# Global attention: three banks for the maximum ring, one bank for the values' sums, and score steps in halves

## The reference

```python
q = _split_heads(x @ Wq + bq, h); k = ...; v = ...
pattern = jnp.einsum('bhid,bhjd->bhij', k, q) * scale
prob = jax.nn.softmax(pattern, axis=-2)
out = jnp.einsum('bhis,bhid->bhsd', prob, v)
return concat @ Wo + bo
```

## Time and profile before

| | |
|---|---|
| time, median of 3 runs | 5361.09 us (5356.98 to 5364.1) |
| profiled execution, its own time | 5343.82 us |
| its span | 5342.2 us |
| TensorE busy | 4731.0 us (89%) |
| VectorE busy | 3525.2 us (66%) |
| GpSimd busy | 2700.6 us (51%) |
| ScalarE busy | 2177.9 us (41%) |

### The profile page before, as it was taken

The page is one execution under the profiler, slowest core; times in us unless marked ns, Lnnn a source line. Parts: engine busy times, 40 slices in busy tenths (PEclk is TensorE's granted clock), DMA queues, the critical chain, the costliest instruction groups (busy, mean ns, idle before and its releaser), DMA issues.

```text
span 5342.2 us, 67966 instructions
## 1 busy us (share of the span) xinstructions
PE 4731.0 (89%) x21552; PEld 2824.3 (53%) x21552; DVE 3525.2 (66%) x4540; ACT 2177.9 (41%) x3392; POOL 2700.6 (51%) x1140
## 2 busy tenths in 40 slices
PE   5899999999999598788859999999999985987978
PEld 3455555555454375566634555555555543765656
DVE  4878778778775553454467787787787755544544
ACT  2334434434433264355323343344344333643553
POOL 0456556556557264255205565565565562642652
PEclk8999999999999798999979999999999997988989
DMA  1000000000000100000010000000000001000000
GB/s 39 5 5 1 5 5 1 5 5 1 5 2 1 52 1 33 17 1 2 32 35 5 5 1 5 5 1 5 5 1 5 2 1 52 1 33 17 1 33 16
DMA packets 78786, 59.19 MB, mean 11 GB/s; under 512 B 41304, under 2 KB 75392, under 8 KB 78464
## 3 DMA queue, kind: packets, MB, share of 16 engines
q1 hardware_dynamic: 78464, 54.93, 3.3%
HBM read 50.45 MB, written 4.19 MB: 10 GB/s over the span
## 4 chain that ended last, share of the span: by engine, by line
POOL 43%; issue 33%; PE 12%; DVE 7%; ACT 3%; POOLq 1%; DMA 1%; DVEq 0%; SPq 0%; ACTq 0%
POOL accp L607 33%; PE psum L1437 4%; POOL lp L629 4%; POOL accp L603 3%; PE psum L1312 2%; ACT lp L744 1%; POOL rnorm L619 1%; DVE lnr L388 1%; POOL qk_u L624 1%; PE psum L1450 1%; DVE qk_w L997 1%; DVE lneg L1011 1%; PE psum L358 1%; DVE ssq L985 1%; PE psum L1358 1%
## 5 line engine op out<-in xcount | busy, mean ns | idle before, releaser
L607 POOL TENSOR_TENSOR accp<-accp,prob 128x1024 f32<-128x1024 f32 x640 | 1596.2, 2494 | 791.9 <-ACT prob L702 758.0
L702 ACT ACTIVATE prob<-psum 128x1024 f32<-128x1024 f32 x1024 | 1040.9, 1024 | 1829.4 <-PE psum L1215 1626.7
L884 DVE TENSOR_REDUCE mx<-psum 128x1 f32<-128x512 f32 x1920 | 1249.5, 685 | 463.2 <-PE psum L1192 429.4
L1226 PE MATMUL psum<-prob,vv 128*64 128x512 f32 x4096 | 994.9, 607 | 0.0
L1214 PE MATMUL psum<-qhh,klh 128*128 128x512 f32 x2048 | 836.4, 408 | 41.2 <-issue 21.5
L1215 PE MATMUL psum<-qlm,kh 65*128 65x512 f32 x2048 | 823.9, 402 | 0.0
L1192 PE MATMUL psum<-klh,qhh 128*128 128x512 f32 x1920 | 721.0, 431 | 73.5 <-DVE mx L884 68.0
L1192 PEld LDWEIGHTS psum<-klh,qhh 128*128 128x128 f32 x1920 | 335.7, 189 | 534.7 <-DVE mx L884 382.7
L1226 PEld LDWEIGHTS psum<-prob,vv 128*64 128x64 f32 x4096 | 249.3, 136 | 513.0 <-issue 391.4
L607 POOL TENSOR_TENSOR accp<-prob 128x1024 f32<-128x1024 f32 x64 | 153.2, 2394 | 697.6 <-ACT prob L702 692.6
L1214 PEld LDWEIGHTS psum<-qhh,klh 128*128 128x128 f32 x2048 | 395.8, 193 | 207.8 <-issue 98.5
(11 more groups left out here) (158 smaller groups left out, 6709.8 us busy)
## 6 DMA issues: line engine op xcount, KB each, us to landing
rot_l<-const_rot SPq DMA_DIRECT2D x6, 2048.0 KB, 8.1
wqkv_l<-L_ffn_wqkv SPq DMA_DIRECT2D x12, 768.0 KB, 9.5
w_l<-L_ffn_w SPq DMA_DIRECT2D x8, 682.0 KB
tok<-L_attn_x SPq DMA_DIRECT2D x32, 128.0 KB, 2.2
out<-tok SPq DMA_DIRECT2D x32, 128.0 KB, 1.7
wo_l<-L_ffn_wo SPq DMA_DIRECT2D x6, 512.0 KB, 10.0
w_l<-L_ffn_w SPq DMA_DIRECT2D x4, 640.0 KB
wqk<-L_attn_Wq SPq DMA_DIRECT2D x32, 64.0 KB, 2.2
```

Source lines behind the costliest of these rows:

```text
L607: pool.tensor_tensor(acc_p[cp][:], first[:], prob[kt % PRING][:], ALU.add).then_inc(pool_sum, 1)
L702: act.activation(prob[t % PRING][:], psum[:, S_BANK + 2 * (t % 2):S_BANK + 2 * (t % 2) + 2, :].rearrange("p a b -> p (a b)"), ACT.Exp, sca ...
L884: dve.tensor_reduce(mx4[:, j // CHUNKS, j % CHUNKS:j % CHUNKS + 1], ps, AX_X, ALU.max).then_inc(ring_free, 1)
L1226: mm = pe.matmul(psum[j * DH:(j + 1) * DH, O_BANK + cp, :], vv[:, kt, s * DH:(s + 1) * DH], prob[t % PRING][:, j * T:(j + 1) * T], start=( ...
```

## The change

- The ring gets a third bank: `RING = 3`, banks 5, 6 and 7. Places are taken modulo 3; a pair takes 147 places, for which the turn of head 0 takes two places and that of head 1 one (`TURN_PLACES`).
- The values' sums have one bank (4) for both blocks of queries. ScalarE reads it out into a new buffer `o_raw[cp]` in SBUF (`read_out`): block 0 behind the exponential of step 17, block 1 behind the projection that follows the head. The value products of the next block wait for that read-out (`o_free`). `normalise` multiplies `o_raw` by the reciprocal, and counts `oT_ready`, for which the output tiles and the next read-out into the same buffer wait.
- A score step is two entries of the list, one for each half. The tiles of a group are dealt in quarters, one quarter in front of each half. With five maximum products the group reads M S M S' M T M M T' V V'; with four maximum products and two output tiles (O) it reads M S M M S' M T O O T' V V', where it was M M S S' M M T T' O O V V'.

```diff
+RING = 3
+TURN_PLACES = (2, 1)
+RING_PAIR = 2 * (RING_MAX + CP) + sum(TURN_PLACES) + V_ITEMS + WO_ITEMS
+        o_raw = [sb(f"o_raw{i}", [P, T], at=att) for i in range(CP)]
-        S_BANK, O_BANK, M_BANK = 0, 4, 6
+        S_BANK, O_BANK, M_BANK = 0, 4, 5
...
-                n = len(tiles)
-                cut0 = (n + 1) // 3
-                cut1 = cut0 + n // 3
                 if g + 1 < GROUPS:
-                    order += tiles[:cut0] + [("scores", 2 * g + 2)] + tiles[cut0:cut1] + [("scores", 2 * g + 3)] + tiles[cut1:]
+                    for q in range(4):
+                        order += tiles[len(tiles) * q // 4:len(tiles) * (q + 1) // 4]
+                        order.append(("scores", (2 * g + 2 + q // 2, q % 2)))
...
                         act.activation(prob[t % PRING][:], psum[:, S_BANK + 2 * (t % 2):S_BANK + 2 * (t % 2) + 2, :].rearrange("p a b -> p (a b)"),
                                        ACT.Exp, scale=float(ATT_SCALE)).then_inc(exp_done, 1)
+                        if t == KT + 1:
+                            read_out(G, 0)
+                def read_out(G, cp):
+                    act.wait_ge(pv_done, G * STEPS + OFF_S + (cp + 1) * KT)
+                    act.wait_ge(oT_ready, G * CP + cp + 1)
+                    act.activation(o_raw[cp][:], psum[:, O_BANK, :], ACT.Copy).then_inc(o_free, 1)
...
                         exps(head_index(b, hp, hh))
                         project(head_index(b, hp + 1, hh), hh)
+                        read_out(head_index(b, hp, hh), 1)
...
                     dve.reciprocal(rcp[:], ps).then_inc(ring_free, 1)
-                    dve.wait_ge(ring_free, OFF_RING + 2 + rb + i + 1)
-                    dve.wait_ge(pv_done, G * STEPS + OFF_S + (cp + 1) * KT)
+                    dve.wait_ge(ring_free, OFF_RING + RING + rb + i + 1)
+                    dve.wait_ge(o_free, G * CP + cp + 2)
                     for j in range(2):
                         rows = slice(j * DH, (j + 1) * DH)
                         op = dve.tensor_tensor(oT[hh * DH:(hh + 1) * DH, (2 * cp + j) * T:(2 * cp + j + 1) * T],
-                                               psum[rows, O_BANK + cp, :], rcp[rows, :], ALU.mult)
-                    op.then_inc(o_free, 1)
+                                               o_raw[cp][rows, :], rcp[rows, :], ALU.mult)
+                    op.then_inc(oT_ready, 1)
...
-                    return psum[:, M_BANK + r % 2, :]
+                    return psum[:, M_BANK + r % RING, :]
...
-                def scores(G, s, t):
+                def scores(G, s, t, j):
-                    if t >= 2:
+                    if t >= 2 and j == 0:
                         pe.wait_ge(exp_done, G * STEPS + t - 1)
...
-                        mm = pe.matmul(psum[j * DH:(j + 1) * DH, O_BANK + cp, :], vv[:, kt, s * DH:(s + 1) * DH],
+                        mm = pe.matmul(psum[j * DH:(j + 1) * DH, O_BANK, :], vv[:, kt, s * DH:(s + 1) * DH],
                                        prob[t % PRING][:, j * T:(j + 1) * T], start=(kt == 0), stop=(kt == KT - 1))
```

More of the change, by code:

```diff
@@ L278, in head_order @@
             placed = max_places(outs)
-            order = [("scores", 0), ("scores", 1)]
+            order = [("scores", (0, 0)), ("scores", (0, 1)), ("scores", (1, 0)), ("scores", (1, 1))]
             for g in range(GROUPS):
@@ L315, in pair_plan @@
                     rows.append((kind, j, r))
-                    r += kind in IN_RING
+                    r += TURN_PLACES[hh] if kind == "turn" else kind in IN_RING
                 plans.append(rows)
-            assert r == RING_PAIR + (0 if last else RING_PRO - WO_ITEMS)
+            assert RING_PAIR % RING == 0 and r == RING_PAIR + (0 if last else RING_PRO - WO_ITEMS)
             return plans
@@ L711, in _ @@
                         project(head_index(b, hp + 1, hh), hh)
+                        read_out(head_index(b, hp, hh), 1)
                 for hh in range(2):
                     exps(head_index(b, PAIRS - 1, hh))
+                    read_out(head_index(b, PAIRS - 1, hh), 1)
                 phase_end(act, b, PH_ATT)
@@ L848, in _ @@
             dve.wait_ge(su_d, 8)
-            for s, n in ((ring_free, OFF_RING + 2), (dve_sum, OFF_DVE), (o_free, CP),
+            for s, n in ((ring_free, OFF_RING + RING), (dve_sum, OFF_DVE), (o_free, 1), (oT_ready, CP),
                          (ln_c, 1), (ln_done, 2), (ug_done, 2), (y_read, 1), (lo_read, 1)):
@@ L875, in ring_wait @@
                     dve.wait_ge(ring_full, OFF_RING + rb + i + 1)
-                    return psum[:, M_BANK + i % 2, :]
+                    return psum[:, M_BANK + i % RING, :]
                 def proj_v(rb, r, i):
@@ L886, in max_all, with max_neg @@
                 def max_all(rb, r):
-                    dve.wait_ge(ring_free, OFF_RING + 2 + rb + r)
+                    dve.wait_ge(ring_free, OFF_RING + RING + rb + r)
                     dve.tensor_reduce(mx1[:], mx4[:], AX_X, ALU.max).then_inc(mx_red, 1)
-                def max_neg(G, rb, r):
+                def max_neg(G, rb, r, places):
                     ps = ring_wait(rb, r)
                     dve.wait_ge(mrow, G * 16 + 16)
-                    dve.tensor_scalar(nmx[:], ps[0:KT, 0:P], -1.0, None, ALU.mult).then_inc(ring_free, 1)
+                    dve.tensor_scalar(nmx[:], ps[0:KT, 0:P], -1.0, None, ALU.mult).then_inc(ring_free, places)
                 def add_sum(G, cp, j):
@@ L929, in head @@
                         elif kind == "turn":
-                            max_neg(G + 1, rb, r)
+                            max_neg(G + 1, rb, r, TURN_PLACES[hh])
                         elif kind == "values":
@@ L953, in _ @@
                 max_all(ring_base(b, 0), RING_PRO - 1)
-                max_neg(head_index(b, 0, 0), ring_base(b, 0), RING_PRO - 1)
+                max_neg(head_index(b, 0, 0), ring_base(b, 0), RING_PRO - 1, 1)
                 for hh in range(2):
@@ L1193, in max_tile, with turn @@
                               start=True, stop=True).then_inc(ring_full, 1)
-                def turn(G, rb, r):
+                def turn(G, rb, r, places):
                     ps = ring_slot(rb, r)
                     pe.wait_ge(mx_red, G + 1)
-                    pe.transpose(ps[0:KT, 0:P], mx1[:], identf[:]).then_inc(ring_full, 1)
+                    pe.transpose(ps[0:KT, 0:P], mx1[:], identf[:]).then_inc(ring_full, places)
                 def projected(G, items):
@@ L1203, in projected @@
                     pe.wait_ge(pj_dve, G * QK_ITEMS + items)
-                def scores(G, s, t):
+                def scores(G, s, t, j):
                     cp, kt = divmod(t, KT)
-                    if t >= 2:
+                    if t >= 2 and j == 0:
                         pe.wait_ge(exp_done, G * STEPS + t - 1)
                     keys = slice(kt * P, (kt + 1) * P)
[L1211 to L1216, removed]
+                    cols = slice((2 * cp + j) * T, (2 * cp + j + 1) * T)
+                    ps = psum[:, S_BANK + 2 * (t % 2) + j, :]
+                    pe.matmul(ps, klh[s][:, keys], qhh[s][:, cols], start=True, stop=False)
+                    mm = pe.matmul(ps, kh1[s][:, keys], qlm[s][:, cols], start=False, stop=True)
+                    if j == 1:
+                        mm.then_inc(s_full, 1)
                 def values(G, rb, s, t):
@@ L1220, in values @@
                     if s == 0 and t == 0:
-                        pe.wait_ge(ring_free, OFF_RING + 2 + rb + VALUES_READ)
+                        pe.wait_ge(ring_free, OFF_RING + RING + rb + VALUES_READ)
                     pe.wait_ge(exp_done, G * STEPS + t + 1)
@@ L1243, in out_tile @@
                         pe.wait_ge(wo_in, 16 * use)
-                        pe.wait_ge(o_free, G * CP + CP + CP)
+                        pe.wait_ge(oT_ready, G * CP + CP + CP)
                     pe.matmul(ps, wo_p[:, m * P:(m + 1) * P], oT[:, c * T:(c + 1) * T], start=True, stop=True).then_inc(ring_full, 1)
@@ L1252, in head @@
                         if kind == "scores":
-                            if j < 2 and not tail:
-                                projected(G + 1, 2 * j + 2)
-                            scores(G, s, j)
+                            t, half = j
+                            if t < 2 and half == 0 and not tail:
+                                projected(G + 1, 2 * t + 2)
+                            scores(G, s, t, half)
                         elif kind == "max":
@@ L1262, in head @@
                         elif kind == "turn":
-                            turn(G + 1, rb, r)
+                            turn(G + 1, rb, r, TURN_PLACES[hh])
                         elif kind == "proj_qk":
@@ L1283, in _ @@
                 for qt in range(KT):
-                    pe.wait_ge(ring_free, OFF_RING + 2 + ring_base(b, 0) + V_ITEMS + max(qt - 1, 0) * CHUNKS)
+                    pe.wait_ge(ring_free, OFF_RING + RING + ring_base(b, 0) + V_ITEMS + max(qt - 1, 0) * CHUNKS)
```

(2 more changed lines are left out.)

3 lines of the change are left out of this document (1 added, 2 removed).

## The result

The changed kernel takes 5299.5 us (5294.6 to 5301.1, four runs) against 5359.0 us in the same comparison: ratio 0.9886, 95% interval 0.9869 to 0.9903, some 60 us less. The forecast was 5291, a gain of 70. The two profiled executions lie only 45.5 apart (5343.8 and 5298.4, the second put at 5274): that of the kernel before ran 15 under its median, and what is read from the two traces adds up to these 45.

A forecast was written before the change was run, and what follows sets the result against it. TensorE was taken as the bound, losing 9.3 us a pair to the two-bank ring. With 3.3 left, the gain was 89 us, or 51 with GpSimd between; the middle, 70, gave 5291 us, range 5252 to 5331, chance 0.77.

The forecast's parts named there:

- TensorE is the bound and the ring of two its loss: Steady pairs: TensorE busy 96%, losing 9.3 us a pair to late-freed banks; a perfect ring could give 138 us.
- the lock: Normalising: VectorE with two SBUF inputs and GpSimd exclude each other, one waiting for the other's whole instruction; products 1.1 or more.
- the sum: Whole pair: 3.3 of 9.3 us left, gain 6.0, 89 us in all; 51 with GpSimd between the products; middle 70.
- Third bank behind a probability add: Groups of five maximum products: loss falls from 0.54 to 0.3 us, four times a pair; with output tiles, 0.
- Order alone: Score halves and quartered tiles: same products and weight loads, same 0.1 us each side of the values; costs nothing.
- Read-outs: ScalarE's 64 copies of the values' sums, 0.68 us each (0.6 to 0.7), cost nothing; without cover 44 us.
- Normalising from SBUF: What the change pays: products with two SBUF inputs meet GpSimd; 1.5 us a pair mid-head, 0.3 or 3.0 at one border.
- the two ends for the border: Head 0 to head 1: TensorE loses 0.3 us if the second product follows directly, 3.0 if GpSimd's add comes between.
- the walk: Step-by-step timing at the head 0 to head 1 border: VectorE asks at 865.01, ends at 869.8 with GpSimd between.
- At the other border GpSimd is idle: 0: The pair's border other than head 0 to head 1: no GpSimd work, so normalising from SBUF costs 0.
- Mid-head: Normalising inside a head: VectorE meets one GpSimd add; TensorE loses about 0.75 us against 1.04, twice a pair.
- A sign that did not come: TensorE's shown wait for maxima, 4.6 us a pair, was to fall below 2.

The follow-up runs named there:

- the fastest kernel: Changed kernel with the reciprocal left in PSUM, the old places of the maximum products, and one wait and one count behind the normalising products: 5223.7 us, ratio 0.9752.
- the kernel with the PSUM reciprocal: Changed kernel with VectorE's reciprocal written back into the ring's bank, products reading it there, ring place given back behind them: 5240.2 us, ratio 0.9785.
- the shorter fence: Against the kernel with the PSUM reciprocal, same order: `ring_free` on the second product, `oT_ready` counted behind one wait: 5231.5 us, ratio 0.9763.

## Why the prediction was right, point by point

- **TensorE is the bound and the ring of two its loss.** Right. The ring's loss was put at 9.3 us a pair, 138 in all. The kernel that keeps three banks and leaves the lock out gains 135, and with two banks that gain is gone. That 135 lies so near 138 is in part chance: the fastest kernel still waits 21.6 for maxima, and it saves some 20 at the borders of two pairs, which the sum did not have.
- **Third bank behind a probability add.** 0.3 forecast, 0.22 in the trace. In the groups with output tiles 0 forecast and 0 seen.
- **Order alone.** "Nothing" was right for three banks in the sense of the timing, and the experiments say more: with two banks it costs 43 us, with three the intervals with and without it overlap. The change has two ideas, and only the bank is shown to carry it.
- **Read-outs.** Free, as priced. They take 0.60, the lower bound:

```profile
L711 ACT ACTIVATE o_raw<-psum 128x512 f32<-128x512 f32 x64 | 38.3, 598 | 36.5 <-PE psum L1237 35.8
```

The first of a head, in ScalarE's order of time, ends a microsecond before its next exponential begins:

```profile
403.89 1.02 ACT L704 ACTIVATE prob<-psum 128x1024 f32<-128x1024 f32 x1 [1.21 <-PE psum L1225]
405.70 0.60 ACT L711 ACTIVATE o_raw<-psum 128x512 f32<-128x512 f32 x1 [0.78 <-PE psum L1237]
407.36 1.02 ACT L704 ACTIVATE prob<-psum 128x1024 f32<-128x1024 f32 x1 [1.06 <-PE psum L1225]
```

- **Normalising from SBUF.** Right in kind. Of the two ends for the border the lower one is true: at all 14 borders from head 0 to head 1 that have maxima behind them the two products take 4.8 us, GpSimd's add between them, which is the 4.8 of the walk (865.01 to 869.8). The Trainium skill (SBUF — State Buffer, Who interferes with whom: issue order decides who blocks) had this end, and the trace agrees. The walk's price for TensorE, 3.0, measured 2.6 without the clock's fall and 3.3 with it; against the kernel before the border's group grew by 2.9, where the sum had 2.7. But I took the middle of the two ends, 70, which neither of them gives; the mechanism that came true gave 51. That the measured 60 lies near 70 is therefore in part luck.
- **"At the other border GpSimd is idle: 0"** failed where no loop jump lies: from pair 0 to pair 1, and from 6 to 7, GpSimd is at work and the two products meet two adds, 5.69 for the two, four times in the run. TensorE stands 2.21 each time, and with the clock behind it the group takes 9.4 to 12.2 where 6.8 stood, 15 us in all:

```profile
356.72 5.69 DVE L923 TENSOR_TENSOR oT<-o_raw,rcp 64x512 f32<-64x512 f32 x2
```

- **Mid-head** 0.75 was forecast. Before the row below, in head 1, TensorE waits 0.46, and inside it 0.47; for head 0 it is 0.24 and 0.47. So 0.9 and 0.7.

```profile
525.07 1.10 PE L1203 MATMUL psum<-klh,qhh 128*128 128x512 f32 x2 [0.30 <-DVE mx L895]
```

- **The balance,** over all groups of both batches in the two profiled executions, in us:

| groups | number | before | after | saved |
|---|---|---|---|---|
| with output tiles | 52 | 375.8 | 342.8 | 33.0 |
| at the border from head 0 to head 1 | 14 | 74.4 | 114.6 | -40.1 |
| the four of 5.69 above | 4 | 27.3 | 42.0 | -14.7 |
| over a jump of the loop to the next pair | 10 | 184.6 | 168.6 | 16.0 |
| all others | 426 | 2445.4 | 2391.0 | 54.3 |

The first row and the last give 87, where the sum had 14.8 x 6.0 = 89; the border takes 40, where it had 38. The two other rows were in no term of the sum: 15 lost and 16 gained (last section), and that they cancel is luck. In all 48.5; the rest of the kernel takes 3 more.

- **The clock** was not in the sum either. The stall at the border is followed in seven of 14 cases by some microseconds at the lower level, 1.4 us each time.
- **A sign that did not come.** TensorE's shown wait was to fall below 2 us a pair; it is 2.5 in a steady pair (2.17 and 0.31), because the border's alone is 2.2. The other signs came: pairs of 197.8, copies of 0.60, products of 1.67 on the mean and 2.88 at most.

## What to carry to other kernels

When an evacuation is moved from PSUM to SBUF to free a bank, count the SBUF inputs of what reads it next: here a VectorE product that had two waited for whole GpSimd instructions, and two such in a row let one in between (4.8 us for 1.4). Leaving one of the operands in PSUM cost a bank for 1.4 us and was worth 58 us, as much as the whole change. The ring that a late consumer blocked was mended by one more place, and where two ideas come in one change, time each alone: here one of them was worth nothing that shows and the other all. And compare the groups of a whole pair before and after, and not only the waits that were foreseen: 16 us gained and 15 lost lay at a border that the prediction had put at nothing.

## What the runs showed that I had not expected

- TensorE, too, starts late behind a jump back of the hardware loop, with nothing that the profile shows to wait for, and with the third bank that is shorter. Its idle at the ten jumps, first in the kernel before, then in the changed one:

```profile
PE psum L1214 <- issue: 21.5, 10, 2.4
```

```profile
PE psum L1224 <- issue: 12.9, 10, 1.7
```

The four kernels with two banks have 21.5 to 22.4 us there, the eight with three 12.5 to 15.2, whatever their order and their operands. In the kernel before the clock then falls behind each of the ten (0.72 on the mean of 6 us), in the changed one behind two, and is 1.00 behind eight. Both together make the 1.6 us a pair. Why a third bank shortens the start was not tried.

- Behind a jump back of the hardware loop VectorE starts late. From the normalising products to the first maximum it idled 1.7 to 2.2 us in the kernel before and in the changed one, 4.2 to 4.6 in the kernel with the PSUM reciprocal, and 3.2 to 3.7 with the shorter fence, while TensorE's first maximum product had mostly long been done. TensorE's first full group behind the jump takes 8.1 on the mean with the PSUM reciprocal and 7.1 with the shorter fence and the same order, where 6.6 is usual: over ten jumps 9.5 us, about the distance of 5240 and 5231. More semaphore steps at the end of the body go with a longer start; the cause was not tried. The rows of the kernel with the PSUM reciprocal:

```profile
741.77 1.40 DVE L923 TENSOR_TENSOR oT<-o_raw,psum 64x512 f32<-64x512 f32 x2
747.66 3.68 DVE L895 TENSOR_REDUCE mx<-psum 128x1 f32<-128x512 f32 x6 [4.49 <-PE psum L1205]
```

- VectorE's adds took from 1.88 to 2.47 us on the mean from kernel to kernel with the same work, and the places at which they meet GpSimd's moved. A small change of order may pay or cost by that alone, which no run tried by itself, and a walk through a single group could not foresee it.
